# The last dense stage of a two-layer gated transformer block, moved into the block of the attention before it

## The reference, cut to what matters

```python
x = x + tanh(g_xattn[0]) * xattn0(layernorm(x), ctx)     # 32 heads, 8 key groups
x = x + tanh(g_ffn[0])   * ffn0(layernorm(x))            # gated, 1376 wide
x = x + tanh(g_xattn[1]) * xattn1(layernorm(x), ctx)     # keys: context and latents, rms-normed
x = x + tanh(g_ffn[1])   * ffn1(layernorm(x))

def ffn1(xf):                                            # 1024 rows of 512
    base, logits = xf @ base_W.T, xf @ gate_W.T          # 512x512; 28 experts
    top_vals, top_idx = top_k(logits, 2)
    gate_full = scatter(softmax(top_vals), top_idx)      # 1024 x 28, two entries a row
    h = einsum('nd,erd->ner', xf, lora_A)                # 28 experts of rank 8
    h = h * (gate_full * 2.0)[:, :, None]
    return base + einsum('ner,eor->no', h, lora_B)
```

## Time and profile before

| | us |
|---|---|
| median of 3 runs | 1514.88 |
| lowest and highest | 1511.53, 1515.43 |
| the profiled execution | 1515.12 |
| its span (first to last instruction) | 1513.3 |
| PE busy | 1424.4 (94%) |
| DVE busy | 1114.1 (74%) |
| ACT busy | 795.7 (53%) |
| POOL busy | 427.0 (28%) |

### The profile page before, as it was taken

How to read it: one execution, slowest core, us unless ns; L and a number is a source line. 1 busy time by engine, 2 the same in 40 slices (tenths; PEclk the granted TensorE clock), 3 DMA queues, 4 the chain that set the end, 5 groups by cost and what they waited for, 6 DMA issues and landing times. The chain is left out here.

```text
span 1513.3 us, 24457 instructions
## 1 busy us (share of the span) xinstructions
PE 1424.4 (94%) x8064; PEld 1210.9 (80%) x8064; DVE 1114.1 (74%) x2922; ACT 795.7 (53%) x2201; POOL 427.0 (28%) x512
## 2 busy tenths in 40 slices
PE   5999999999899998999999999999999999999889
PEld 4888888887778887788888888888788888887767
DVE  7888888888651535778778778787787787777765
ACT  5667666666320314565565565555555655555521
POOL 4733334442691831121111111111111211112120
PEclk9999999999999999999999999999999999999989
DMA  4111111110230310100101001001001001010001
GB/s 188 71 47 65 64 60 69 69 42 29 84 101 27 85 79 0 70 1 21 50 1 69 0 0 69 0 0 69 0 0 69 0 2 67 16 39 1 1 1 56
DMA packets 14934, 63.76 MB, mean 42 GB/s; under 512 B 1760, under 2 KB 1760, under 8 KB 10656
## 3 DMA queue, kind: packets, MB, share of 16 engines
q1 hardware_dynamic: 14880, 63.07, 11.8%
HBM read 60.97 MB, written 2.10 MB: 42 GB/s over the span
## 5 line engine op out<-in xcount | busy, mean ns | idle before, releaser
L1206 ACT ACTIVATE p<-psum,nb,rq 128x320 f32<-128x320 f32 x256 | 155.1, 613 | 162.4 <-DVE nb L989 162.4
L55 PE MATMUL psum<-w1q_hi,xnT_lo 128*128 128x512 f32 x256 | 107.6, 420 | 6.5 <-DVE pT_lo L954 6.5
L954 DVE TENSOR_TENSOR pT_lo<-psum,pT_hi 128x512 fp32r<-128x512 f32 x128 | 88.2, 690 | 33.1 <-ACT pT_hi L1129 31.4
L985 DVE TENSOR_REDUCE mx<-psum 128x2 f32<-128x640 f32 x128 | 105.1, 821 | 5.6
L434 ACT ACTIVATE p<-psum,nb 128x64 f32<-128x64 f32 x256 | 76.8, 313 | 50.9 <-DVE nb L344 50.8
L919 POOL TENSOR_TENSOR rk<-ssk,rms_eps 128x3 f32<-128x3 f32 x32 | 6.3, 196 | 344.7 <-DVE ssk L1026 344.7
L55 PE MATMUL psum<-w1o_hi,oT_lo 128*128 128x512 f32 x256 | 100.7, 393 | 0.0
L57 PE MATMUL psum<-w1q_hi,xnT_hi 128*128 128x512 f32 x256 | 100.7, 393 | 0.0
L56 PE MATMUL psum<-w1o_lo,oT_hi 128*128 128x512 f32 x256 | 100.5, 393 | 0.0
L57 PE MATMUL psum<-w1o_hi,oT_hi 128*128 128x512 f32 x256 | 100.1, 391 | 0.0
L56 PE MATMUL psum<-w1q_lo,xnT_hi 128*128 128x512 f32 x256 | 99.7, 389 | 0.0
(11 more groups left out here) (250 smaller groups left out, 4804.1 us busy)
## 6 DMA issues: line engine op xcount, KB each, us to landing
raw_q<-in_w0q SPq DMA_DIRECT2D x8, 1024.0 KB, 4.8
raw_o<-in_w0o SPq DMA_DIRECT2D x8, 1024.0 KB, 4.7
raw_q<-in_w1q SPq DMA_DIRECT2D x8, 1024.0 KB, 7.5
raw_o<-in_w1o SPq DMA_DIRECT2D x8, 1024.0 KB, 4.8
raw_kv<-in_w_gu SPq DMA_DIRECT2D x10, 512.0 KB, 3.6
raw_gu<-in_w_gu SPq DMA_DIRECT2D x10, 512.0 KB, 3.6
raw_kv<-in_w0kv SPq DMA_DIRECT2D x8, 515.0 KB, 3.3
raw_kv<-in_w1kv SPq DMA_DIRECT2D x8, 512.0 KB, 5.5
```

The lines of the kernel that those rows point to most:

```text
L55: pe.matmul(out, w[1], m[0], start=start, stop=False)
L954: last = dve.tensor_tensor(k.pT[1][:, kt, 2 * hp:2 * hp + 2, :], bank.rearrange("p (h q) -> p h q", h=2), f(k.pT[0][:, kt, 2 * hp:2 * hp + ...
L985: dve.tensor_reduce(k.mx[:, stat(j)], s_pair(j), AX.X, ALU.max).then_inc(mx_ready, 1)
L1206: last = act.activation(k.p1[:, tile, h, :], s_pair(j)[:, h % 2, :], ACT.Exp, bias=k.nb[:, i:i + 1], scale=k.rq[:, i:i + 1], accum_out=k.r ...
```

## The change

`ffn1_phase` and its block are gone. A class `Ffn1` has its steps, and the `tail` of each engine in `attn1_phase` calls them.

- **Weights.** `split_next` is now also true in the last group, so unit 31 converts two pieces of the expert and gate weight into `w_kv` and four pieces of the base weight into `w_q` (a buffer of the attention). Its low-rank weight is converted by GpSimd alone (`pool_weights`: two casts and two subtractions), into the buffer of `qT`, once unit 31's scores are done.
- **Buffers.** Small tiles lie in `dump`, the copies of the first product and the gated row in `q_raw`, the transposed row in `kT`. The expert and gate product has one bank (1) instead of two, the transposes one (4) instead of two; base products have banks 0, 2 and 3.
- **Order.** The products of tiles 0, 1 and 2 stand between the steps of unit 31's rest. The base product of tile 0 and the first product stand ahead of all its transpositions. From tile 3 on a round is: first product of s, transposes of s - 1, base product of s, low-rank product of s - 1.
- The barrier between the two blocks is gone. The optional phases of `build` are gone too.

Cut to its core:

```diff
+    def weights(kind, g, i):
+        s = piece(kind, i)
+        if kind == "kv" and isinstance(g, int) and g == NKV:
+            c = slice(2 * i, 2 * i + 2)
+            return k.raw_ag[:, c, :], k.w_ag[0][:, c, 0:LR + NEXP], k.w_ag[1][:, c, 0:LR + NEXP]
+        return raw[kind][:, s], flat[kind][0][:, s], flat[kind][1][:, s]
...
-                    split_next = b == BATCH - 1 and nxt
+                    split_next = b == BATCH - 1
...
             def tail(n):
-                for t in (4, 5):
+                ffn1.pool_weights(pool)
+                for t in range(4, NT):
                     ln.pool_rstd(pool, 3, t)
+    def pool_weights(self, pool):
...
+        pool.wait_ge(self.free["scores"], 4 * self.units)
+        pool.iota(k.iota_i, pattern=[[1, NEXP]], base=0, channel_multiplier=0).then_inc(self.iota_set, 1)
+        pool.wait_ge(k.f1_in["o"], 32)
+        pool.tensor_copy(k.w_b[0][:, 0, :], k.raw_o[:, 0:HID])
+        pool.tensor_copy(k.w_b[0][0:low, 1, :], k.raw_o[0:low, HID:2 * HID]).then_inc(self.b_hi, 1)
+        pool.wait_ge(self.b_hi, 1)
+        pool.tensor_tensor(k.w_b[1][:, 0, :], k.raw_o[:, 0:HID], f(k.w_b[0][:, 0, :]), ALU.subtract)
...
...
             def tail(n):
-                for j in range(6):
-                    turn(n, 0, j, alone=True)
-                    if j == 3:
-                        pe.wait_ge(x_added, 2 * (n - 1))
-                        p_v(n, 0, 0, alone=True)
+                ffn1.pe_ag(pe, 0)
+                ffn1.pe_base(pe, 0)
+                turn(n, 0, 0, alone=True)
+                turn(n, 0, 1, alone=True)
+                ffn1.pe_ag(pe, 1)
+                turn(n, 0, 2, alone=True)
+                turn(n, 0, 3, alone=True)
+                ffn1.pe_base(pe, 1)
+                turn(n, 0, 4, alone=True)
+                turn(n, 0, 5, alone=True)
+                pe.wait_ge(x_added, 2 * (n - 1))
+                p_v(n, 0, 0, alone=True)
+                ffn1.pe_ag(pe, 2)
                 p_v(n, 0, 1, alone=True)
-                for i in range(2):
-                    ln.pe_turn(pe, 3, 4 + i, ln_bank(4, i))
-                for j in range(2):
-                    out(n, 0, j)
+                ffn1.pe_base(pe, 2)
+                ffn1.pe_hgT(pe, 0)
+                out(n, 0, 0)
+                ffn1.pe_low_rank(pe, 0)
+                ffn1.pe_hgT(pe, 1)
+                ln.pe_turn(pe, 3, 4, ffn1.ln_bank(4))
+                out(n, 0, 1)
+                pe.wait_ge(x_added, 2 * n - 1)
+                ln.pe_turn(pe, 3, 5, ffn1.ln_bank(5))
+                ffn1.pe_low_rank(pe, 1)
+                for s in range(3, NT):
...
+                    ffn1.pe_ag(pe, s)
+                    ffn1.pe_hgT(pe, s - 1)
+                    ffn1.pe_base(pe, s)
+                    if s < NT - 1:
+                        ffn1.pe_low_rank(pe, s - 1)
+                ffn1.pe_hgT(pe, NT - 1)
+                ffn1.pe_low_rank(pe, NT - 2)
+                ffn1.pe_low_rank(pe, NT - 1)
+    def pe_ag(self, pe, s):
...
+            pe.wait_ge(self.free["kv"], self.conv["kv"] * (NKV + 1))
+            pe.wait_ge(self.free["exp"], 4 * self.units - 1)
+    def pe_base(self, pe, s):
...
+            pe.wait_ge(self.free["q"], self.conv["q"] * (NKV + 1))
```

More of the change, by code:

```diff
@@ L893, in loop @@
         tail(NKV * BATCH)
+    ffn1 = Ffn1(k, sem, ln, free={"kv": kv_wlo, "q": q_wlo, "exp": exp_done, "scores": s_full, "w_kv": kv_full,
+                                  "turned": t_split, "x": x_added, "whi": kv_whi}, conv=CONV, units=UNITS)
     with nc.Block() as block:
@@ L943, in w_lo @@
             def w_lo(kind, g, i):
[L944 removed]
+                src, hi, lo = weights(kind, g, i)
                 dve.wait_ge(whi[kind], CONV[kind] * g + i + 1)
[L946 to L947 removed]
+                dve.tensor_tensor(lo, src, f(hi), ALU.subtract).then_inc(wlo[kind], 1)
             def t_lo(n, b, j):
@@ L1140, in w_hi @@
             def w_hi(kind, g, i):
-                s = piece(kind, i)
+                src, hi, _ = weights(kind, g, i)
                 act.wait_ge(arrived[kind], 16 * g + 16)
-                act.activation(flat[kind][0][:, s], raw[kind][:, s], ACT.Copy).then_inc(whi[kind], 1)
+                act.activation(hi, src, ACT.Copy).then_inc(whi[kind], 1)
             def body(g, first, nxt):
@@ L1579, in build, with ffn1_views, cut, twice @@
-def build(nc, d, out, phases=("attn0", "ffn0", "attn1", "ffn1")):
+    k.ffn1_load = load
+def ffn1_views(k):
+    k.raw_ag = k.raw_kv[:, 0:CH * (LR + NEXP)].rearrange("p (c n) -> p c n", c=CH)
+    k.w_ag = [w[:, :].rearrange("p (c n) -> p c n", c=CH) for w in k.w_kv]
+    k.w_base = k.w_q
+    k.w_b = [w[:, :, :, :].rearrange("p t h q -> p t (h q)") for w in k.qT]
+    spare = k.kT[0][:, :, :].rearrange("p b n -> p (b n)")
+    k.hgT = [spare[:, i * 512:(i + 1) * 512].rearrange("p (u c n) -> p u c n", u=2, c=2) for i in range(2)]
+    k.ag, k.hg = k.q_raw[:, :, 0:256], k.q_raw[:, :, 256:256 + LR]
+    small = k.dump[:, :, :].rearrange("p a b -> p (a b)")
+    at = [0]
+    def cut(n, dtype=None):
+        ap = small[:, at[0]:at[0] + n]
+        at[0] += 16 * math.ceil(n / 16)
+        return ap.bitcast(dtype) if dtype else ap
+    def twice(n, dtype=None):
+        return [cut(n, dtype) for _ in range(2)]
+    k.iota_i, k.iota = cut(NEXP, mybir.dt.int32), cut(NEXP)
+    k.top, k.idx, k.idxf = twice(8), twice(8, mybir.dt.uint32), twice(2)
+    k.gap, k.eg, k.pr = twice(1), twice(1), twice(4)
+    k.ga, k.gb, k.gm = twice(NEXP), twice(NEXP), twice(NEXP)
@@ L1581, in build @@
+def build(nc, d, out):
     k = Kernel()
@@ L1652, in layouts @@
+        with ExitStack() as scope:
+            ffn0_buffers(k, scope, sb, pair)
+            ffn0_phase(nc, k, sem, ln)
+        with ExitStack() as scope:
+            attn1_buffers(k, scope, sb, pair)
+            ffn1_views(k)
+            attn1_phase(nc, k, sem, ln)
 def layouts(inputs):
```

427 lines of the change are left out of this document (204 added, 223 removed).

## The result

| | before | after |
|---|---|---|
| median of 4 runs, us | 1514.12 | 1505.75 |
| lowest and highest of after | | 1503.71, 1506.73 |
| the profiled execution | 1515.12 | 1505.85 |
| its span | 1513.3 | 1504.0 |
| PE busy | 1424.4 (94%) | 1421.5 (95%) |

The ratio after to before is 0.9946, 95% interval 0.9931 to 0.9961: 8.4 us less, where 10.9 were forecast. The time lies in the range, 1.75 us above the forecast of 1504.0.

What follows compares the result with a forecast made beforehand. PE was taken as the bound, with 19.4 us of idle time and half clock in the tail; losses of 8.45 afterwards leave 10.9 less, so 1515.12 becomes 1504.2, median 1504.0, range 1500 to 1508.5.

Steps and rivals of the forecast that it cites:

- One sign of being wrong: The prediction would be wrong if, among other signs, the dense steps were longer than 5.9 us.
- last unit longer: Last attention unit: one added activation ahead of the last probability copies shows as 0.35 us, bounds 0 and 0.7.
- wait for the exponentials: After the last scores, PE waits 0.4 us for the third pair's exponentials, which free the bank.
- wait before the base product, bare: Tile 0's base product waits at least 2.4 us for DVE's fourth base piece, if nothing else disturbs DVE.
- GpSimd's part of it: Before tile 0's base product, GpSimd's low-rank weight work delays DVE by 1.6 us, range 0 to 3.0.
- second and third turn: In the attention's rest behind the base product, small leftover waits at these turns: 0.3 us.
- last gated row: At the end, tile 7's gated row has too little PE work in front of it: 1.2 us of wait.
- clock: Around the wait before the base product, one fall to half clock costs 2.2 us, bounds 0 and 5.7.
- How much there is to win: From last score to last dense product: 59.4 us of PE work in 78.75, so 19.4 idle or half clock.
- its own row: Base piece on DVE that met GpSimd at a cost of 0.38 us; judged to speak neither way on the lock.
- fourth rival: Attention tail: dense products only push the chain back, only the seam's 5.0 us is won: 1510.1, chance 0.06.
- two cases: Tail: one clock fall gives 1504 (1501.5 to 1506.5), chance 0.60; clock holding gives 1500 to 1501.5, chance 0.15.

Runs made afterwards that it cites:

- second profile of the changed kernel: The changed kernel run again with no edit: median 1503.51 us, ratio 0.9915 to the kernel before.
- GpSimd later: Changed kernel, but GpSimd starts on the low-rank weight only when DVE's last base piece is done: 1500.93 us, ratio 0.9898 to the kernel before.
- the run without the interleave: Changed kernel with the old order of the tail and DVE's four base subtractions behind the attention's last low parts: 1515.78 us, ratio 1.0004 to the kernel before.
- the run with GpSimd behind: The run without the interleave, with GpSimd's low-rank weight made behind the inverse deviations of tiles 4 and 5: 1511.59 us, ratio 0.9968 to the kernel before.
- the best order: Changed kernel with all four base pieces on DVE ahead of the fourth row maximum in unit 31: 1500.38 us, ratio 0.9897 to the kernel before.
- together with the earlier pieces: Changed kernel with base pieces earlier on DVE and GpSimd's low-rank weight held behind them: 1501.94 us, ratio 0.9900 to the kernel before.

## Why the prediction was right, step by step

The mechanism held at each place that was named. The base product starts 3.2 us after the first product ends, released by the fourth base piece. PE has no idle time over 1 us behind it and 0.91 before the last gated row. The mean clock from 1431 to 1457 is 0.87, and the last product ends at 1500.83 instead of 1499. One sign of being wrong came in part: from tile 3 on the steps take 6.16, 6.21, 5.84 and 5.80 us (starts 1468.16, 1474.32, 1480.53, 1486.37 and 1492.17), two of them over 5.9. PE has no wait in these two; they carry the last layer-norm transposes, four each, at about 0.1. The sizes, against the second profile of the changed kernel (no fall of the clock) and against the first (one fall there):

| term | forecast, us | measured, us |
|---|---|---|
| last unit longer | 0.35 | 0.44 |
| wait for the exponentials | 0.4 | 0.62 |
| wait before the base product, bare | 2.4 | 1.77 |
| GpSimd's part of it | 1.6 | 1.44 |
| second and third turn | 0.3 | 0 |
| last gated row | 1.2 | 0.91 to 0.92 |
| clock | 2.2 | 2.5 in one profile, 0 in the other |
| sum | 8.45 | 7.7, or 5.2 without the fall |

- **How much there is to win.** The tail without a fall is 65.18, its three waits are 0.62 + 3.21 + 0.92 = 4.75, so PE's work took 60.4 us where 59.4 had been added up. This 1.0 too little made the room for a gain too large, and the losses were forecast 0.8 too high. The two nearly cancel, which is luck: tail and last unit gave 78.75 - 67.70 - 0.44 = 10.6 us, forecast 10.9.
- **The bare wait** was mis-sized by 0.6. With GpSimd later, the fourth base piece is done 4.0 us after the last score product (1432.15 to 1436.15) where 4.2 were forecast. The first product ends 2.3 us after the scores and not 1.8: the wait for the exponentials is 0.2 longer, and a product lasts 0.23 beyond its price when nothing follows it, since that price was read from start to start (1432.77 to 1434.44 is 1.67, not 1.44).
- **GpSimd beside DVE.** 1.6 was taken between two rows, half of the meetings at each, and came out at 1.44. It was right in size by an average that hides its kind. What a meeting cost follows what was left of GpSimd's work: 0.25 for the end of one instruction, 0.90 where 1.10 of one was left, 2.03 where 2.53 of both subtractions was left, in the run without the interleave. GpSimd's two took 1.26 and 1.34 there, so it is one waiting for the other and not both running slower. Why the cost is 0.2 to 0.5 less than what was left isn't shown; a row of two scalings is merged. The Trainium skill, SBUF — State Buffer, section "SBUF: two separate sides", calls the shared port pair "an exclusive lock, not a bandwidth split", and says that whichever starts first holds it for the whole instruction. The traces agree with it, 2.71 us for a pair of 0.68. It names VectorE operations with two SBUF inputs or in a two-port mode, and the row maximum, whose one input is in PSUM, stays at 0.81. The prediction said that its own row spoke neither way and priced the rule as the upper end; the lock was the right reading. The wait stayed at 3.2 and not 5.4 because the wait without GpSimd was shorter, the row maximum and the addition into x, which read PSUM, ran beside GpSimd at their usual 0.81 and 0.74, and part of each instruction met was already over.
- **The casts.** They take 0.61 to 0.69, not the bound of 1.29. So GpSimd was done 1.2 us earlier than by that bound.
- **The tail behind the base product.** No wait of over 0.2 from there to the last row: the forecast 0.3 was too much, and "PE nearly always with work" held. The fourth rival (the dense products only push the chain back, so only the seam is won, 1510.1) is refuted by that: its waits don't come again. Its price for the seam was right, 5.0 us in the run with GpSimd behind. The interleave carries the other part: the tail falls from 74.02 to 65.28 with GpSimd later, and to 62.80 in the best order.
- **The clock.** Three stretches of 17.0 us together were forecast for before and are in both its profiles. For after one fall of 5.7 us worth 2.2 was forecast; it was 6.8 long and worth 2.52, in one profile of two. In the first the fall came, in the second not, with the same program and waits of 3.22 and 3.21. The prediction gave one fall and none to two cases, and the same program did both behind the same wait, so which of them came was chance. The five later executions of the changed kernel have mean clocks of 0.998, 0.998, 0.994, 0.995 and 0.994 and times of 1501.73, 1501.68, 1504.57, 1503.51 and 1504.36: the two at 0.998 are 2 to 3 us faster. So the spread goes with the clock, but a mean over 1500 us doesn't say where the falls lay; in the first profile two of them lay between 580 and 598.
- **What is missing.** For the profiled execution 1504.2 was forecast and 1505.85 measured. Of these 1.65 us 0.3 are the terms above and 1.34 were lost before the last unit: 2.3 us to the two falls of the clock some 800 us ahead of it, which no term held, less 1.0 by which this execution was ahead elsewhere. That the result came within 1.75 us of the forecast is in part luck: the profiled execution of the changed kernel that had none of these falls took 1501.73, 2.5 below the forecast for it and still in the range.

Still open: what decides whether the clock falls behind a wait of about 3 us. The waits of 1.77 (fell, for 3.4 us), 2.67 (fell), 3.21 (held) and 3.22 (fell) are no order by length, and one profile of each can't tell a rule from chance.

## What to carry to other kernels

Before work of the next stage is put between the steps of this one, look at which of its operands is ready last, and move that one's conversion ahead of whatever the hand-offs already wait for: it was worth 2.4 us of the tail here (65.18 to 62.80) for a few moved lines. Don't leave GpSimd elementwise work on SBUF to start "as soon as it can" at a place where VectorE is the one everybody waits for: in the version without the interleave it had eaten the whole gain, 4.2 us. When you hold it back, look at what VectorE does next: behind the base pieces alone it gave 1.44 us, and together with the earlier pieces it met the scalings and gave nothing. And test a change of two parts in parts: half of this one measured as nothing, for a reason that belonged to neither half's idea.

## What the runs showed of the hardware

- VectorE and GpSimd hold each other up until most or all of the other's instruction is over, in both directions: 0.68 became 2.71 and 0.16 became 0.37 to 0.55 on VectorE, 1.26 became 1.61 on GpSimd. A VectorE operation on two elements a partition is hit as well, an operation that reads PSUM wasn't (0.81 beside a running subtraction).
- Stretches at the lower clock lasted from 3.4 to 10.2 us; one of 6.8 us in which PE was busy for 5.57 cost 2.5. The Trainium skill, TensorE: Matmul & The Clock Gate, section "Part 1: The HAM clock gate (the "warmup" mystery)", calls the number of slow matmuls at a kernel's start "run-variable"; the two profiles of one program show that in the middle of a kernel a fall can come or stay away too.
- 48 matmuls whose results nobody reads made a kernel faster: 1506.08 against 1507.79, ratios to before of 0.9930 (0.9914 to 0.9947) and 0.9942 (0.9926 to 0.9959). The ratios' intervals overlap; the two traces (2.1 us of tail) and the mean clocks of the other executions (0.997 and over against 0.995 and under) are what separates them.
